# Attending two tiles of keys in one block of matmuls, with twelve buffers of probabilities, in a one-core decoder layer

## What is computed

```
x = x + attn(layernorm(x))        # 16 heads of 16, softmax(q k / 4 + ALiBi bias), then out_w
x = x + xattn(layernorm(x), ctx)  # one head over 77 context rows
x = x + moe(layernorm(x))         # top 2 of 8 experts, 256 -> 1024 -> 256, relu
```

## Time and profile before

| what | us |
|---|---|
| median of 3 runs | 1608.52 |
| lowest and highest run | 1606.69, 1613.93 |
| span of the profiled execution | 1607.6 |
| PE busy in it | 1552.3 (97%) |
| DVE busy | 1189.6 (74%) |
| ACT busy | 934.6 (58%) |
| POOL busy | 387.4 (24%) |

### The profile page before, as it was taken

The page is one execution under the profiler, slowest core; times in us unless marked ns, Lnnn a source line. Parts: engine busy times, 40 slices in busy tenths (PEclk is TensorE's granted clock), DMA queues, the critical chain, the costliest instruction groups (busy, mean ns, idle before and its releaser), DMA issues.

```text
span 1607.6 us, 31234 instructions
## 1 busy us (share of the span) xinstructions
PE 1552.3 (97%) x10542; PEld 963.5 (60%) x10542; DVE 1189.6 (74%) x2409; ACT 934.6 (58%) x1786; POOL 387.4 (24%) x462
## 2 busy tenths in 40 slices
PE   5899999999999999999999999999999999999997
PEld 3433443344554444445434443439999999999997
DVE  5888878888877788787877777713354788888885
ACT  3156656677556767664765756772222466666663
POOL 6201120002110041210013100142134334344443
PEclk9799999999999999999999999999999999999998
DMA  6561351232151450314414333234556666766763
GB/s 181 110 126 24 74 122 23 23 43 34 38 99 52 70 86 13 44 41 83 70 51 73 44 106 132 68 130 128 158 179 204 190 199 198 208 191 199 210 192 102
DMA packets 92672, 173.41 MB, mean 108 GB/s; under 512 B 13236, under 2 KB 51124, under 8 KB 92385
## 3 DMA queue, kind: packets, MB, share of 16 engines
q1 hardware_dynamic: 75376, 143.69, 35.2%
q0 software_dynamic: 15744, 26.54, 7.6%
q10 hardware_dynamic: 1392, 1.18, 0.4%
HBM read 133.69 MB, written 37.29 MB: 106 GB/s over the span
## 4 chain that ended last, share of the span: by engine, by line
PE 90%; DVE 4%; ACT 2%; issue 2%; DMA 1%; POOL 0%; SPq 0%; ACTq 0%; DVEq 0%; POOLq 0%
PE ps L1395 16%; PE ps L1183 15%; PE ps L1209 14%; PE ps L1169 13%; PE ps L1138 8%; PE ps L1421 5%; PE ps L1281 2%; PE ps L1315 2%; PE ps L1212 2%; DVE rmax L1632 2%; PE ps L1172 2%; ACT prob L1439 1%; PE ps L1228 1%; PE ps L1383 1%; PE ps L1296 1%
## 5 line engine op out<-in xcount | busy, mean ns | idle before, releaser
L1632 DVE TENSOR_REDUCE rmax<-ps 128x1 f32<-128x512 f32 x960 | 621.2, 685 | 175.4 <-PE ps L1212 86.4
L1439 ACT ACTIVATE prob<-ps 128x512 f32<-128x512 f32 x1024 | 560.8, 601 | 308.2 <-PE ps L1169 157.7
L1209 PE MATMUL ps<-stacked_k,stacked_q 112*128 112x512 bf16 x1024 | 392.1, 390 | 11.4 <-DVE rmax L1629 3.8
L1169 PE MATMUL ps<-stacked_q,stacked_k 115*128 115x512 bf16 x1024 | 358.7, 381 | 3.0 <-ACT prob L1439 1.6
L1183 PE MATMUL ps<-prob,values 128*32 128x512 f32 x2048 | 273.6, 606 | 6.8 <-ACT prob L1439 6.8
L1395 PE MATMUL ps<-xiT,w_now 128*128 128x128 f32 x2272 | 267.5, 275 | 0.0
L1209 PEld LDWEIGHTS ps<-stacked_k,stacked_q 112*128 112x128 bf16 x1024 | 99.5, 99 | 279.2 <-DVE rmax L1632 184.2
L1395 PEld LDWEIGHTS ps<-xiT,w_now 128*128 128x128 f32 x2272 | 262.7, 192 | 1.3
L1169 PEld LDWEIGHTS ps<-stacked_q,stacked_k 115*128 115x128 bf16 x1024 | 97.7, 98 | 152.1 <-ACT prob L1439 67.9
L2060 POOL DMA_INDIRECT out<-yo,xi x71 | 114.9, 1618 | 244.6 <-DVE yo L1935 219.8
L1559 ACT ACTIVATE hidT<-ps,b 128x128 f32<-128x128 f32 x284 | 80.1, 364 | 97.0 <-PE ps L1395 97.0
(11 more groups left out here) (222 smaller groups left out, 1954.7 us busy)
## 6 DMA issues: line engine op xcount, KB each, us to landing
w_now<-in_w SPq DMA_DIRECT2D x71, 1024.0 KB, 5.3
stacked_q<-parts_of_rows SPq DMA_DIRECT2D x90, 128.0 KB, 6.1
stacked_k<-parts_of_rows SPq DMA_DIRECT2D x90, 128.0 KB, 6.7
xi<-expert_rows SPq DMA_DIRECT2D x71, 130.0 KB, 2.2
w<-in_w SPq DMA_DIRECT2D x8, 1024.0 KB, 9.2
parts_of_rows<-q_part SPq DMA_DIRECT2D x21, 256.0 KB, 6.7
parts_of_rows<-k_part SPq DMA_DIRECT2D x21, 256.0 KB, 7.0
xr<-in_x POOLq DMA_DIRECT2D x4, 1024.0 KB, 9.8
```

What stands on the lines that cost most here:

```text
L1169: m = e.matmul(ps[:, bank, :], ka[i][0:ROWS, hh, kt * P:(kt + 1) * P], qa[i][0:ROWS, hh, ch * BANK:(ch + 1) * BANK], start=True, stop=True)
L1209: m = e.matmul(ps[:, bank, :], qa[i][0:MAX_ROW, hh, qt * P:(qt + 1) * P], ka[i][0:MAX_ROW, hh, kc * BANK:(kc + 1) * BANK], start=True, sto ...
L1439: e.activation(prob[:, u % NPROB, :], ps[:, score_bank(u), :], ACT.Exp).then_inc(sem["exp"], 1)
L1632: e.tensor_reduce(rmax[:, G % 2, hh * NT + qt, kc:kc + 1], ps[:, p.bank("max", *k), :], AX.X, ALU.max).then_inc(sem["maxed"], 1)
```

## The change

`attend_two()` attends everything in `waiting`. It is called only when two tiles wait, after the third unit of the next tile (the fourth in the last group), and `waiting` now lives across groups: a group's last two tiles are attended after the next group's third unit. What used to follow a group's last attend (`ended`, `finish`, `spread`, `prefetch`, first loads of the experts) moved with it. `behind()` is left out after one unit in eight in place of one in four. `prob` grows from 8 to 12 buffers, 24 KB, and the descriptors' part shrinks from 16 KB to 8 KB.

```diff
-NPROB = 8
+NPROB = 12
...
+    waiting = []
+
+    def attend_two():
+        while waiting:
+            G, ch, kt = waiting.pop(0)
+            add("attend", G, ch, kt)
+        if kt < NT - 1:
+            return
+        if ch == NCH - 1:
+            now["ended"] += 1
+        closing.append(finish(G, ch))
+        step_on(closing)
+        if ch == NCH - 1:
+            spread_when_ready()
+            if G < LAST:
+                add("prefetch", G)
+            if G == LAST - 1:
+                add("load", 0)
+                add("load", 1)
...
-        waiting = []
         for ch in range(NCH):
             for kt in range(NT):
                 for hh in range(HG):
                     unit(ch, kt, hh)
-                    if hh == (3 if G == LAST else 2) and waiting:
-                        c_, k_ = waiting.pop(0)
-                        add("attend", G, c_, k_)
-                        if k_ == NT - 1:
-                            closing.append(finish(G, c_))
-                            step_on(closing)
+                    if hh == (3 if G == LAST else 2) and len(waiting) == 2:
+                        attend_two()
                     else:
                         step_on(closing)
                         behind(G // NG)
                     maximum(0)
-                waiting.append((ch, kt))
-        add("attend", G, *waiting.pop(0))
-        now["ended"] += 1
-        closing.append(finish(G, NCH - 1))
-        step_on(closing)
-        spread_when_ready()
-        if G < LAST:
-            add("prefetch", G)
-        if G == LAST - 1:
-            add("load", 0)
-            add("load", 1)
+                waiting.append((G, ch, kt))
+    attend_two()
...
-    nc = bacc.Bacc("TRN2", target_bir_lowering=False, num_devices=1)
+    nc = bacc.Bacc("TRN2", target_bir_lowering=False, num_devices=1, dynamic_dma_scratch_size=8192)
```

## The result

The changed kernel takes 1622.41 us (median of 4 runs, 1620.03 to 1624.04); the kernel before, measured beside it, 1610.32. The ratio is 1.0076, 95% interval 1.0054 to 1.0099: **slower** by some 12 us (0.8%), where 1585 us (1574 to 1602) had been forecast. The profiled execution has 1618.2 us between its first and last instruction, 10.6 more than before.

A forecast was written before the change was run, and what follows sets the result against it. PE was taken to bound the attention, before and after. -22.8 for merges, -6.5 for ends of groups and +6 for DVE running dry gave -23.3 us: span 1607.6 to 1584.3, metric 1585 us, range 1574 to 1602.

The forecast's parts named there:

- Part 1: Attends on PE: 120 merges of two tiles into one block save 0.19 us each, 22.8 us less.
- Part 2: Ends of groups: attending the last tile behind the next group's scores removes PE's waits, 6.5 us less.
- Part 3: Twelve buffers of probabilities: no cost, and what makes merging possible.
- Part 4: Moved steps (loads, ACT's copy of the output bank, side work asked for sooner): all hidden, 0.
- Part 5: Half the descriptor space, for GpSimd's indirect stores: 0, with bounds 0 and 2 us.
- Part 6: DVE runs dry during blocks of two attends: 6 us more, between 0 and 22.
- Rival D: Slower: DVE idle above 1.56 us per pair makes DVE's total exceed the present stretch; 1630 at 1.75; chance 0.07.
- Rival B: DVE binds in most of the attention at 1.5 us idle per pair: about 1601, or 1594; chance 0.18.
- C: Rival: the block's second tile does not stream on PE, loads or accumulation standing in the way: 1597 to 1604; chance 0.11.

The follow-up runs named there:

- e1: The changed kernel with one tile attended at a time again, all else kept: 1604.77 us, ratio to the kernel before 0.9966.
- e9: The kernel before with only the twelve buffers of probabilities and the smaller descriptor space added: 1606.60 us, ratio 0.9984.
- e10: The changed kernel, same order, with only the exponentials halved (256 of 512 columns), a probe that leaves out work: 1612.30 us.

## Why the prediction was wrong

**Part 1, merging: right, and somewhat too low.** 22.8 us was forecast, 28.8 came, or 0.23 for a merge, above the 0.21 that was taken for the most. A block's third and fourth passes follow after 0.43 rather than 0.45, and the last group's seven merges, counted at nothing, shorten PE's work as well, though ACT's pace takes that back as stalls. The Trainium skill's rule on row groups (TensorE: Matmul & The Clock Gate, "The mechanism") does not hold here: the second tile's loads ran under matmuls on the same rows, in groups of four of 0.13 us. The same section also lets loads into the background weight buffer run ahead of matmuls, which the prediction left out; whether that is what happens here no run shows.

**Part 2, ends of groups: the wait goes as forecast, the gain only in part.** Waits at attends fell from 6.8 to 0.3 us; alone (e1 against e9) that was worth 3 us, by one trace of each, with more of the lower clock in e1.

**Part 3 failed.** "No cost" looked at the buffers of probabilities and never at the three score banks. ACT drains those inside the block and stands idle (2.07 us at 516.51); afterwards PE outruns it. Stalls before scores are 16.6 us more, and e10 shows that they are ACT's. No rival had ACT in it.

**Part 4** had 0. Other stalls rose by 4.3, which is unexplained. The rest of the kernel fell by 5.8: 2.1 us of idle time ahead of the experts went, where side work had come sooner, and 2.9 us belong to part 5.

**Part 5 was right that there is no cost**: e9, ratio 0.9984. With the larger `prob` it even went with 2.9 us less at the kernel's end. (Its working counted the 71 stores; GpSimd issues 64 more indirect DMAs, `expert_rows`, from 561.6 us on.)

**Part 6 is the step that decided.** It took 6 us for DVE running dry; the stalls before max matmuls grew by 32.6. The mechanism was named, the size was wrong, and the reason lies in how it was sized: by totals. Setting 852 us of DVE against 901 of PE asks whether DVE can do its work in the stretch. It can, and is idle for 187.0 us in front of its reductions. The idle time per pair was not the mistake: with the 1.08 us measured the same sum gives 873, still below 901, and so no loss at all. But the order is fixed and there are two banks. What counts is whether the reductions of two tiles, beside DVE's own side work, fit in the time between one block and the next at every single block. Where they don't, PE waits, and where DVE is ahead, nothing is given back: 42 tight stretches of 127 hold 36.9 us. So PE and DVE both lose time, and neither total shows it. Rival D was on the right side, and its price came from the same totals, with a threshold of 1.56 us per pair; it had a chance of 0.07 because of it. Rival B, at 1.5 per pair, saw the same idle time (1.35 here) and still had the kernel faster. C did not happen.

The sum with the measured terms: -28.8 for merges, -7.2 of stalls at attends, +32.6 before max matmuls, +16.6 before scores, +4.3 others, -5.8 in the rest, -1.1 before the first score: +10.6, the difference of the two spans.

## What to carry to other kernels

A longer uninterrupted block on the bound engine is paid for by its helpers: before merging, compare the block's length with what their banks hold (here two reductions of 0.63 us against 1.86) and then the helpers' work between two blocks with the time between them, block by block. Helpers at 60 to 80% of a stretch are not slack to be spent, when the order is fixed. And where matmuls' records overlap, measure waits from start to start; busy shares hid 29 us of gain and 46 of loss here.

## What the runs showed of the hardware

- Going to 32-column tiles and back costs 0.23 us in all: 0.09 on entry, 0.02 after the first pass (0.45 to the next in place of 0.43) and 0.12 on leaving (0.54 from the last pass's start to the next matmul). It is paid per block, not per matmul.
- Removing stalls in one of two queues that PE serves in a fixed order raises them in the other: 26.3 to 32.3 before scores with half reductions, 46.6 to 57.9 before max matmuls with half exponentials (one run each).
- Waits of 1.88 and 3.69 us, 5 us apart, went with 10.2 us of the lower clock (granted clock 0.73 over the 19 us around them). The clock also fell without any gap on PE: in e1 it fell for 6.8 us at 545.9, in the middle of 16 matmuls with eight columns each.
- Twelve buffers and 8 KB for descriptors in place of eight and 16 KB went with 6 in place of 9 us between GpSimd's last store and the end of the span.
